# An MoE block's last stage with one batch entry in each partition: attention's sum goes through memory into that layout

## What is computed

```
y  = einsum(x, w1[subject of the batch entry])       # 32x32 per entry, mixes the entry's 32 tokens
x1 = x + attention(y)                                # 16 heads, causal, quantised projections
h  = einsum(x1, w2[condition of the batch entry])    # mixes tokens again
out = x1 + moe(h)                                    # 16 experts, the best 2 per token, SiLU(g)*u, F = 96
```

## Time and profile before

| | |
|---|---|
| median of 3 runs (lowest, highest) | 418.84 us (416.54, 424.53) |
| the profiled execution | 420.85 us |
| its span, first to last instruction | 419.1 us |
| busy: PE / DVE / ACT / POOL | 313.0 / 254.8 / 247.3 / 220.6 us |
| moved by DMA | 68.89 MB in 76,900 packets |
| mean granted TensorE clock | 0.893 of full speed |

### The profile page before, as it was taken

The page is one execution under the profiler, slowest core; times in us unless marked ns, Lnnn a source line. Parts: engine busy times, 40 slices in busy tenths (PEclk is TensorE's granted clock), DMA queues, the critical chain, the costliest instruction groups (busy, mean ns, idle before and its releaser), DMA issues.

```text
span 419.1 us, 10285 instructions
## 1 busy us (share of the span) xinstructions
PE 313.0 (75%) x3281; PEld 233.8 (56%) x3281; DVE 254.8 (61%) x876; ACT 247.3 (59%) x588; POOL 220.6 (53%) x263
## 2 busy tenths in 40 slices
PE   4586998989898989998765500999999999991000
PEld 1343465748575656666453400898998989980000
DVE  2554387899999999896765381244444444440865
ACT  9253578787888989886864400466666666660000
POOL 8153224233584748575667874176766767663000
PEclk9998799999999999999995855699999999996555
DMA  6624555544556472726666846565666667613999
GB/s 200 184 87 111 111 107 123 124 94 100 141 152 136 128 183 62 189 61 169 141 179 173 211 136 266 133 186 169 184 183 183 171 176 181 177 59 96 373 400 335
DMA packets 76900, 68.89 MB, mean 164 GB/s; under 512 B 41002, under 2 KB 65967, under 8 KB 76720
## 3 DMA queue, kind: packets, MB, share of 16 engines
q1 hardware_dynamic: 65008, 43.76, 42.8%
q0 software_dynamic: 7296, 20.02, 13.1%
q10 hardware_dynamic: 4544, 4.46, 3.1%
HBM read 35.36 MB, written 30.62 MB: 157 GB/s over the span
## 4 chain that ended last, share of the span: by engine, by line
PE 21%; issue 21%; POOL 16%; DVE 14%; DMA 10%; ACT 8%; SPq 5%; DVEq 2%; POOLq 1%; ACTq 1%
POOL y_d L562 11%; SPq L416 4%; DMA arena<-y_d 4%; POOL routed L516 4%; PE bank L1235 2%; PE bank L1299 2%; PE bank L1146 2%; PE bank L1263 2%; PE bank L1248 2%; DMA arena<-kT 2%; PE bank L1184 2%; DMA qT<-in_L_cond_weights,ids 2%; PE bank L1169 1%; ACT cen L599 1%; DVE amax L839 1%
## 5 line engine op out<-in xcount | busy, mean ns | idle before, releaser
L562 POOL DMA_INDIRECT y_d<-cen,di x79 | 77.7, 983 | 47.1 <-issue 33.6
L516 POOL DMA_INDIRECT routed<-hrow,posi x64 | 65.2, 1019 | 16.5 <-issue 16.2
L1091 DVE SCALAR_TENSOR_TENSOR kT<-kT,hrow,bank 128x96 f32<-128x96 f32 x79 | 24.8, 314 | 74.5 <-ACT kT L775 74.5
L1405 PE MATMUL bank<-arena,qT 128*128 x316 | 66.2, 333 | 0.0
L497 POOL TENSOR_TENSOR sc<-sc,mx 128x512 f32<-128x512 f32 x32 | 33.7, 1053 | 48.4 <-DVE mx L900 48.1
L1405 PEld LDWEIGHTS bank<-arena,qT 128*128 128x128 f32 x316 | 50.9, 195 | 0.4 <-issue 0.4
L1399 PE MATMUL bank<-ident,hrow 128*128 128x128 f32 x158 | 31.3, 281 | 22.6 <-DMA hrow<-routed 22.6
L1415 PE MATMUL bank<-arena,sc 96*128 x158 | 47.3, 381 | 0.0
L780 ACT ACTIVATE cen<-bank 128x256 f32<-128x256 f32 x79 | 30.3, 384 | 23.5 <-PE bank L1415 23.4
L770 ACT ACTIVATE qT<-bank 128x256 f32<-128x256 f32 x79 | 29.9, 378 | 23.5 <-PE bank L1399 23.5
L1399 PEld LDWEIGHTS bank<-ident,hrow 128*128 128x128 f32 x158 | 22.6, 145 | 31.0 <-DMA hrow<-routed 23.1
(11 more groups left out here) (177 smaller groups left out, 691.9 us busy)
## 6 DMA issues: line engine op xcount, KB each, us to landing
hrow<-routed SPq DMA_DIRECT2D x79, 129.0 KB, 2.6
arena<-y_d SPq DMA_DIRECT2D x16, 512.0 KB, 12.5
v_d<-v_sb SPq DMA_DIRECT2D x8, 544.0 KB, 4.0
vx<-v_d SPq DMA_DIRECT2D x32, 136.0 KB
X<-in_x SPq DMA_DIRECT2D x8, 512.0 KB, 4.1
out_x<-X ACTq DMA_DIRECT2D x16, 256.0 KB, 9.3
arena<-kT SPq DMA_DIRECT2D x60, 64.0 KB
arena<-in_L_ffn_gate_w SPq DMA_DIRECT2D x4, 384.0 KB, 3.8
```

What stands on the lines that cost most here:

```text
L516: g_.indirect_dma_start(routed, bass.IndirectOffsetOnAxis(ap=posi[g % 2][:, t, k:k + 1], axis=0), hrow[:, g % 2, t, k, :], None).then_inc( ...
L562: g_.indirect_dma_start(y_d, bass.IndirectOffsetOnAxis(ap=di[:, n:n + 1], axis=0), ye[n], None, bounds_check=Y_ROWS - 1, oob_is_err=False) ...
L1091: v.scalar_tensor_tensor(out=hh[n % 2], in0=sg[n % 2], scalar=xe[n][:, D + 1:D + 2], in1=bank[2 + n % 2][:, F:2 * F], op0=ALU.mult, op1=AL ...
L1405: last = t_.matmul(bank[2 + n][:, 0:2 * F], xeT[n][:, c, :], gu[:, c, bass.ds(expert(k - 1), 1), :].rearrange("p o f -> p (o f)"), start=( ...
```

## The change

`x1` is now stored to a new memory tensor `x1_d`, group by group, by SyncE in the attention loop (`put_x1`, called last in each iteration, for group `it - 3`). In the expert loop ScalarE's queue loads it back in four pieces (`load_x1`, after steps 8, 16, 24 and 32) into the same tile `X`, but with batch entry p in partition p: 32 tokens of 256 numbers, contiguous in memory. The views `y_v` and `out` of the last stage follow that layout, so that a partition's contiguous run is 4 KB in a load and 2 KB in a store. `FIN` stays 16. VectorE waits for the reload ahead of the last stage.

```
-FIN = TILES // TF
+FIN = SEQ // TF
+XB = 4
+XBT = SEQ // XB
...
+    x1_d = nc.dram_tensor("x1_d", [TOKENS, D], fp32, kind="Internal").ap()
...
-    out_v = out.rearrange("(t b) s d -> (b s) t d", b=BT)
-    y_v = y_d.rearrange("(t p k) d -> p t k d", p=P, k=TOPK)
+    y_v = y_d.rearrange("(p t k) d -> p t k d", t=SEQ, k=TOPK)
+    x1_v = x1_d.rearrange("(t p) d -> p t d", p=P)
+    x1_b = x1_d.rearrange("(p t) d -> p t d", t=SEQ)
...
+            def put_x1(g):
+                if absent(g):
+                    return
+                wait(sp, x1_ok, g, 2, 2)
+                sp.dma_start(x1_v[:, g * TG:(g + 1) * TG, :], X[:, g * TG:(g + 1) * TG, :]).then_inc(x1_put, 16)
+
             def iteration(it):
                 put_v(it - 1)
                 spread_v(it - 1)
...
                 next_x(it + 2)
                 spread_k(it)
+                put_x1(it - 3)
...
-            sp.wait_ge(out_put, 16 * (TILES // TF))
+            sp.wait_ge(out_put, 16 * FIN)
...
+            def load_x1(m):
+
+                if m == 0:
+                    act.wait_ge(x1_put, 16 * GROUPS)
+                    act.wait_ge(hT_ready, 2 * GROUPS)
+                act.dma_start(X[:, m * XBT:(m + 1) * XBT, :], x1_b[:, m * XBT:(m + 1) * XBT, :]).then_inc(x1_in, 16)
+
             for k in range(EXPERT_TILES + LAG):
                 step(k, k % DEEP, k // DEEP, None)
+                if k % DEEP == 0 and 1 <= k // DEEP <= XB:
+                    load_x1(k // DEEP - 1)
...
-                act.dma_start(out_v[:, q * TF:(q + 1) * TF, :], X[:, q * TF:(q + 1) * TF, :]).then_inc(out_put, 16)
+                act.dma_start(out[:, q * TF:(q + 1) * TF, :], X[:, q * TF:(q + 1) * TF, :]).then_inc(out_put, 16)
...
+            dve.wait_ge(x1_in, 16 * XB)
             for q in range(FIN):
                 dve.wait_ge(fin_in[q], 16)
```

More of the change, by code:

```diff
@@ L223, in build_in @@
     fin_ok, out_put = sem("fin_ok"), sem("out_put")
+    x1_put, x1_in = sem("x1_put"), sem("x1_in")
     def wait(eng, s, g, per_group, nth, lag=0):
```

## The result

The changed kernel takes 436.31 us (median of 4 runs, 433.34 to 438.38) beside 417.69 us for the kernel before (4 runs, 410.96 to 424.53): a ratio of 1.0504, interval [1.0422, 1.0587]. A second comparison, on another occasion and with 23 runs of the kernel before, gave 1.0348 [1.0298, 1.0397]; the two intervals do not meet. Ratios and intervals come from a comparison of the fast runs alone and the medians from all runs, so that the two need not agree (the medians give 1.045 here and 434.87 / 418.47 = 1.039 in the second comparison). The profiled executions agree with the second ratio: 433.8 against 419.1 us of span, 1.035. The profiled execution of the changed kernel took 435.57 us.

What follows compares the result with a forecast made beforehand. Bound: TensorE in the expert loop, DMA in the last stage, and between attention and experts a gap behind GpSimd's scatter into `routed`. Terms +17.2 - 2.1 + 0.5 = +15.6 on 420.85 gave 436.5, said 436 us; range 427 to 444.

Steps and rivals of the forecast that it cites:

- The order on SyncE: Before the expert loop: SyncE's wait for group 7's residual holds back the weights; TensorE starts +17.2 us later (+7.4 to +21.7).
- the store ahead of the first piece: SyncE's queue: the last store's 512 KB precede the first weight piece, +1.1 us, between 0 and 1.5.
- the padding with the scatters behind it: Gap before the expert loop: GpSimd's padding scatter catches one weight piece, +4.0 us, between 0 and 6.0.
- the other pieces: Weight loads: first pieces meet fewer scatters, later ones as many as before; taken as 0, between 0 and -3.5 us.
- the scatter's delay: GpSimd's scatter, slowed by weight traffic: costs nothing, ending some 15 us before it would be missed.
- The register load: TensorE's load of the expert list after the last weight, no longer covered: 2.5 us, between 1.3 and 4.6.
- The last stage: Final loads and stores: longer runs save 4,096 packets at 8.7 ns each, -2.1 us, ends 0 and -2.2.
- The stores in the attention loop: Five stores between `spread_k` and `put_v` put back `put_v` and `vx`: +0.5 us, ends 0 and 3.
- The reloads: Four reloads issued by ScalarE in the expert loop, where it has room: 0 us, ends 0 and 3.2.
- The reserve: Rival: weights still arrive by about 258 us, chain under 26 us; about 419 us, no change; chance 4%.
- The attention loop held up by 10 us: Rival: `vx` late in every iteration, by 2 us in five of them; +10, about 446 us; chance 10%.
- The far-apart rows: Rival: last-stage loads with partitions 64 KB apart read slowly; +22, about 458 us; chance 4%.

Runs made afterwards that it cites:

- wait alone: Kernel before plus only a SyncE wait in iteration 10 for group 7's late residual, nothing stored or reloaded: 432.25 us, ratio 1.0342.
- short wait: Kernel before plus only a SyncE wait in iteration 9 for group 6's late residual: 420.27 us, ratio 1.0046.
- pieces at once: Changed kernel, SyncE's wait kept, but the ten weight transfers issued without waiting for each other's landing: 422.52 us, ratio 1.0076.
- five stores alone: Kernel before plus only the stores of groups 0 to 4, between `spread_k` and `put_v`, read by nobody: 421.29 us, ratio 1.0040.

## Why the prediction was right, and which terms were off

It said 436 us, from a sum of 436.5 for the profiled execution; that took 435.57, and the medians are 436.31 and 434.87.

*The order on SyncE* was nearly the whole of it, and its mechanism came as described: first gate piece at 231.83 us (232.1 said), last weight landed at 275.85 (277.2), first transposes at 277.88 (279.7), a delay of 15.4 us (17.2). The wait alone reproduces 12.8 of the 15.6 us by which the transposes come later after the residual, and undoing the order takes the delay away. Of its corrections, the store ahead of the first piece costs 4.71 - 3.31 = 1.4 us (1.1 said), the padding with the scatters behind it 4.9 (4.0 said), and the other pieces come out at 44.0 - 40.0 - 1.4 - 4.9 = -2.3 us, where I had taken 0 between 0 and -3.5. The errors partly cancel, here and in the sum: the delay was 1.8 us too long, the last stage's gain 1.0 us too large. That the sum missed by only 0.9 us is in part luck. That the padding and the weights meet was seen from the one side only: the weights are slowed, but when weights still move beside it the padding is slowed as well, and the last scatter behind it lands 2.6 us later after its issue in the short wait and 3.8 in the pieces at once. I had called the scatter's delay free; for the change itself it is, since the weights come later still.

*The register load* is 1.52 us, and 2.0 from the last landing to the transposes (2.5 said). The word by word scaling from SyncE's quiet row, 1.3, came nearest.

*The last stage* is the term that was mis-sized: -2.1 said, -1.1 measured. The price per packet, 8.7 ns, was read from the packets' recorded durations. These came out as worked out: from 411 to 426 us, 67.5% of 240 us over 4.13 MB / 4,096 = 1,008 packets is 161 ns (160.7 by the prices in the prediction), for stores 86 ns (84.7). But the records of different queues overlap, by 1.06 before and 1.04 after, so that a shorter record need not be time saved (argued from these shares, not tested). Both queues' bytes over the 15 us went from 398 to 413 GB/s, 3.8%, which over 12.6 MB is 31.7 - 30.5 = 1.2 us. Per packet saved the measured 1.1 us are 1.1 x 16 / 4,096 = 4.3 ns.
From the overhead of about 3 cycles per packet in the Trainium skill's "DMA: Bandwidth & Descriptors", section "Why small descriptors are slow (HBM only)", I had estimated 4.0 ns and 1.0 us. The measured time fits this estimate and not my reading of the row.

*The stores in the attention loop* cost about 1.7 us [0.3 to 3.1, from the ratio of the five stores alone], not 0.5, inside the ends of 0 to 3. *The reloads* show no cost that can be told from the spread of the expert loop.

*The rivals.* The reserve did not hold: the chain from the late start took 44.0 us, not under 26. The attention loop held up by 10 us is out: the stores cost it about 1.7. The far-apart rows read no slower than the contiguous ones: 413 GB/s against 398, loads and stores together, at a pitch of 64 KB.
The Trainium skill's "DMA: Bandwidth & Descriptors", section "Latency and other measured facts", shows hardly a loss at a pitch of 512 KiB and a clear one from 2 MiB on. These runs agree, as far as 64 KB can show it.

## What to carry to other kernels

When a step is put into a queue that works through its list in order, look at what the list holds behind it, above all at its end, where empty iterations used to run ahead of the pipeline: a wait that costs nothing in the loop may hold up the next phase's loads. Work out the reserve of what stands behind (here 14.9 us against 29) before pricing the step itself. And a transfer that nobody needs for 100 us belongs in the phase that has the room: with stores and reloads both in the expert loop the same layout costs nothing that can be measured, and may be a little faster than the kernel before (0.9949 [0.9910, 0.9988], 0.998 by the medians).

## What the runs showed of the hardware that I had not expected

TensorE's register load of 14 words takes 4.56 to 4.68 us in the six profiles in which it starts 1.8 to 3.2 us after GpSimd's padding scatter was issued. It takes 2.97 us in the short wait, where it lies later within that scatter's 10.3 us, and 1.52 to 1.54 us in the other five. Busy DMA engines alone do not make it long: in the changed kernel the first `xe` loads run beside it at a DMA share of 1.08, against 0.94, and it takes 1.52 us. What in the scatter makes it long is not shown.

```profile
275.90:277.45 1.55, 0.00 (x0) 0.00 (x0) 0.00 (x0) 0.00 (x0) 0.00 (x0) 0.50 1.08 343
```

And a piece of 384-byte runs that meets the padding's scatter takes 8.0 to 8.3 us in three profiles, where the others take 3.2 to 4.2 (4.7 behind a store). The scatter is slowed too: it lands 8.4 to 9.2 us after its issue there, against 7.2 before.
